# Inverse width DFT of a spectral convolution as four 64x64 TensorE tiles per product instead of one 128x128 product

## The reference

```python
xf = jnp.fft.rfft2(x, norm='forward')
top = jnp.einsum('bixy,ioxy->boxy', xf[:, :, :hm0, :hm1], w1)
bot = jnp.einsum('bixy,ioxy->boxy', xf[:, :, -hm0:, :hm1], w2)
out_fft = jnp.zeros((b, cout, h, w // 2 + 1), dtype=xf.dtype)
out_fft = out_fft.at[:, :, :hm0, :hm1].set(top)
out_fft = out_fft.at[:, :, -hm0:, :hm1].set(bot)
return jnp.fft.irfft2(out_fft, s=(h, w), norm='forward')
...
x = x + _L0_conv_ref(_ln_c(x), ...)
t = _to_tokens(x)
t = t + _L0_ffn_ref(_ln_t(t), ...)
```

## Time and profile before

| what | value |
|---|---|
| median of 3 runs (lowest, highest) | 591.72 us (589.74, 591.88) |
| the profiled execution, its own time | 587.68 us |
| its span in the trace | 585.9 us |
| mean granted TensorE clock | 0.962 |
| TensorE matmul busy | 528.1 us, 90% |
| VectorE busy | 344.6 us, 59% |
| ScalarE busy | 300.3 us, 51% |
| GpSimd busy | 114.7 us, 20% |

### The profile page before, as it was taken

How to read it: one execution, slowest core, us unless ns; L and a number is a source line. 1 busy time by engine, 2 the same in 40 slices (tenths; PEclk the granted TensorE clock), 3 DMA queues, 4 the chain that set the end, 5 groups by cost and what they waited for, 6 DMA issues and landing times.

```text
span 585.9 us, 25109 instructions
## 1 busy us (share of the span) xinstructions
PE 528.1 (90%) x11076; PEld 472.0 (81%) x11076; DVE 344.6 (59%) x815; ACT 300.3 (51%) x838; POOL 114.7 (20%) x240
## 2 busy tenths in 40 slices
PE   8978997999965999978999999979999999767997
PEld 8978987899964985767888999969998888656873
DVE  2758997734437936773545455435555455569726
ACT  4557997643377502454444444424445777667100
POOL 4000000000034000001333333553331033461000
PEclk9999998999998899998999999979999999978979
DMA  8940882070000000000000023430000244500007
GB/s 347 369 144 2 303 326 96 3 287 1 2 4 2 2 22 0 1 1 2 4 5 3 4 51 74 109 65 6 3 3 4 40 75 80 101 9 1 2 2 288
DMA packets 50260, 41.69 MB, mean 71 GB/s; under 512 B 44998, under 2 KB 45126, under 8 KB 48934
## 3 DMA queue, kind: packets, MB, share of 16 engines
q1 hardware_dynamic: 49304, 38.51, 20.5%
q0 software_dynamic: 704, 1.18, 0.9%
q10 hardware_dynamic: 144, 0.39, 0.2%
HBM read 27.49 MB, written 4.19 MB: 54 GB/s over the span
## 4 chain that ended last, share of the span: by engine, by line
PE 70%; DVE 16%; ACT 5%; POOL 4%; issue 3%; SPq 1%; DMA 0%; POOLq 0%; ACTq 0%; DVEq 0%
PE PS L755 38%; PE PS L724 5%; DVE RB L990 5%; PE PS L483 4%; PE PS L614 3%; PE PS L674 3%; PE PS L584 3%; PE PS L435 2%; PE PS L462 2%; PE PS L539 2%; POOL RE L393 2%; POOL RCD L396 2%; PE PS L492 2%; DVE sums L1032 1%; PE PS L684 1%
## 5 line engine op out<-in xcount | busy, mean ns | idle before, releaser
L755 PE MATMUL PS<-RE,conv_sb 128*64 128x64 f32 x6048 | 231.2, 230 | 4.3 <-DVE RE L1131 3.9
L755 PEld LDWEIGHTS PS<-RE,conv_sb 128*64 128x64 f32 x6048 | 209.1, 139 | 26.4 <-DVE RE L1131 4.6
L880 ACT COPY PS<-convb_sb 128x64 f32<-128x64 f32 x504 | 108.2, 215 | 112.8 <-DVE RE L1143 89.7
L1143 DVE SCALAR_TENSOR_TENSOR RE<-PS,RCD 128x64 f32<-128x64 f32 x252 | 56.7, 225 | 58.0 <-PE PS L755 50.4
L405 POOL COPY RCD<-RE 128x128 f32<-128x128 f32 x126 | 37.4, 297 | 154.3 <-DVE RE L1143 154.2
L1143 DVE SCALAR_TENSOR_TENSOR RE<-PS,RE 128x64 f32<-128x64 f32 x126 | 32.6, 259 | 28.3 <-PE PS L755 26.9
L1143 DVE SCALAR_TENSOR_TENSOR RE<-PS,RB 128x64 f32<-128x64 f32 x126 | 28.4, 225 | 28.1 <-PE PS L755 20.2
L818 ACT COPY RB<-PS 32x256 f32<-32x256 f32 x64 | 40.5, 633 | 7.5 <-PE PS L523 6.7
L990 DVE COPY RB<-PS 32x256 f32<-32x256 f32 x64 | 40.3, 630 | 5.7 <-PE PS L523 4.9
L539 PE MATMUL PS<-RE,RB 128*64 128x64 f32 x1024 | 33.3, 227 | 5.1 <-DVE RCD L999 2.5
L483 PE MATMUL PS<-warm 128*128 128x128 bf16 x468 | 34.3, 239 | 3.9 <-DVE warm L908 1.4
(11 more groups left out here) (116 smaller groups left out, 715.0 us busy)
## 6 DMA issues: line engine op xcount, KB each, us to landing
RE<-wspec SPq DMA_DIRECT2D x8, 2048.0 KB, 8.5
RA<-x_in SPq DMA_DIRECT2D x8, 512.0 KB, 7.4
RCD<-x_in SPq DMA_DIRECT2D x1, 4096.0 KB, 13.7
out<-RA SPq DMA_DIRECT2D x8, 512.0 KB, 2.9
RCD<-RB SPq DMA_DIRECT2D x58, 64.0 KB, 2.6
RE<-RCD SPq DMA_DIRECT2D x32, 80.0 KB, 2.6
conv_sb<-conv_w SPq DMA_DIRECT2D x1, 768.0 KB, 20.0
w_sb<-w SPq DMA_DIRECT2D x2, 264.0 KB
```

The lines of the kernel that those rows point to most:

```text
L755: m = pe.matmul(conv_bank(s, u, c)[o:o + OC], conv_sb[:, s, d, o:o + OC], prev, start=False, stop=(d == 2), skip_group_check=True)
L880: act.copy(banks_of, convb_sb[:, s:s + 1].unsqueeze(2).to_broadcast([P, c1 - c0, n])).then_inc(s_seed, 1)
L1143: dve.scalar_tensor_tensor(out=state[:, state_slot(s, u), b0:b1, 1:1 + HO], in0=conv_bank(s, u, c), scalar=0.0, in1=row_at(SRC[s], s, q, u ...
```

## The change

`dft_w_back` calls a new function `quad` in place of one 128x128 product. For each block it makes four products of 64x64: row half a of the block and of the table, column half o of the block. The zeros of the table are left out. Row half a now writes to bank a of the pair, so that the pair no longer holds whole blocks one after the other, but the first 64 pixels' columns of all eight blocks in one bank and the second in the other. The residual add reads the pair in that order and RC in the same order as before. Waits, signals and the order of the engines stay as they were.

```diff
+            def quad(bank, n, lhs, table):
+
+                for a in range(2):
+                    rows = slice(MO * a, MO * (a + 1))
+                    for o in range(2):
+                        cols = slice(MO * o, MO * (o + 1))
+                        m = pe.matmul(PS[cols, bank + a, MO * n:MO * (n + 1)], lhs[rows, cols], table[rows, rows],
+                                      start=True, stop=True)
+                return m
+
...
                 for n in range(8):
-                    m = pe.matmul(blk(dft_slot(g), n), blk(RB, 8 * g + n), inv_w, start=True, stop=True)
+                    m = quad(4 + 2 * (g % 2), n, blk(RB, 8 * g + n), inv_w)
                 m.then_inc(s_if1, 1)
...
             for g in range(8):
                 dve.wait_ge(s_if1, g + 1)
-                x1 = RC[:, 1024 * g:1024 * g + 1024]
-                dve.tensor_tensor(x1, dft_slot(g), x1, ALU.add).then_inc(s_res, 1)
+                x1 = RC[:, 1024 * g:1024 * g + 1024].rearrange("p (n a w) -> p n a w", a=2, w=W)
+                dve.tensor_tensor(x1, dft_slot(g).rearrange("p (a n w) -> p n a w", a=2, w=W), x1,
+                                  ALU.add).then_inc(s_res, 1)
```

## The result

The changed kernel takes 587.0 us (median of 20 runs, 583.37 to 589.39), the kernel before, timed beside it, 591.44 us (586.62 to 592.81). The medians lie 4.4 us apart. The ratio on record, which is not simply that of the medians, is 0.994 with an interval of 0.992 to 0.996: 3.5 us less, with 2.4 to 4.7 us in the interval, and that is what I go by. The forecast was 6.6 us.

A forecast was written before the change was run, and what follows sets the result against it. The prediction took TensorE to bound the stage; 5.2 us saved over groups 0 to 5 plus 1.45 us at the end made 6.6 us, so 591.7 - 6.6 = 585.1 us, range 581.0 to 589.0 us.

The forecast's parts named there:

- the floor per record: Rival in the group products: 0.0207 us is a floor of feeding records; 3.9 us saved, 587.8 us; chance 0.20, shared.
- What bounds the stage: First product to projection: TensorE bounds its 20.91 us, until ScalarE's drain (1.01 us per group) or VectorE's add (1.23) is next.
- 0.0146 us per record by the rule of columns: Group products: the larger column count, weights or moving, sets a round of four 64x64 tiles, 0.059 us.
- The gaps: Between products and turns in each group: 0.15 us after a turn stays; 0.20 us taken from products to a turn.
- No drain: Rival at switches between row and quarter tiles: gaps of 0.03 us, 1.7 us more saved, 583.4 us; chance 0.07.
- The add in runs of 64: VectorE's residual add, reading banks in runs of 64: nothing taken; at the strided add's cost, some 1.7 us.
- the end of the stage: Start of group 6 to the projection: 3.70 us instead of 5.15, 1.45 us saved, the add becoming the bound.
- TensorE must also be fed: Feeding 64 more records of each kind per group in the stage: nothing taken; one stop would eat 2.35 us.
- The clock: Rival in the stage: the granted clock falls to half, slower by 5.1 us, 596.8 us; chance 0.05.
- No overlap of the row halves: Rival in the group products: only column halves overlap, 0.029 us per record, gain gone, 592.1 us; chance 0.12, shared.
- a floor, or a single stop or fall of about 3 us: Joint case in the stage: floor of 0.0207 us per record, or one stop or clock fall; near 588 us, chance 0.20.

The follow-up runs named there:

- the mixed tiles: Changed kernel with groups 1, 3 and 5 as row tiles, 16 clock matmuls written as 4; stage 15.74 us, ratio 0.9938 to the kernel before.
- row tiles only: Changed kernel with two 64x128 row tiles per product in place of four 64x64 tiles; stage 18.84 us, ratio 0.9953 to the kernel before.
- the sweeps: Changed kernel plus ten sweeps of 64x64 tiles behind the last product, 64 or 96 moving columns, results unused; sweeps took some 18.5 us in both.
- group 4 or every second group put back: Changed kernel with group 4, or groups 0, 2, 4 and 6, back to 128x128 products; stage 15.91 or 17.59 us, ratio 0.9909 or 0.9953.
- 37 records fewer ahead: Changed kernel with 50 clock matmuls far ahead of the stage written as 13 longer ones; stage 16.79 us, ratio 0.9936 to the kernel before.

## Why the prediction was right, and where it was not

The forecast was faster, 585.1 us in a range of 581.0 to 589.0; the time is 587.0 us. That it lies in the range is in part luck: 3.5 us came of the 6.6 us of the sum, and the range reached up to 589.0 us for the floor per record, which did not come. By the steps of the prediction:

- **What bounds the stage**: right for the kernel before. Shortening the products shortened the stage, and neither drain nor add became the bound inside the loop.
- **0.0146 us per record by the rule of columns**: right. (1.16 - 0.218) / 63 = 0.0149 us, with a median record of 218 ns in the changed kernel. The floor of 0.0207 us does not exist for single records; that rival falls, though its 3.9 us is near the measured 3.5 us. Periods of 1.73 us rather than 2.1 us tell them apart. The row tiles confirm the rule a second time, with 128 columns of weights, to within 6%.
- **The gaps**: right. 1.09 us per group against 1.12 us forecast: 1.09 - 63 x 0.0149 = 0.15 us, less than my 0.20. No drain falls as a rival for this change: the turn still holds 0.64 us. The Trainium skill (TensorEngine Tiling (Array Packing), Key Properties) has TensorE drain at a change of tiling mode, and the trace agrees: 0.64 us for a turn between other forms, 0.50 us between row tiles.
- **The add in runs of 64**: right, 1.23 us as before, and so is the end of the stage where no stop disturbs it: from group 6 to the projection 158.58 - 154.90 = 3.68 us with the mixed tiles, 3.70 forecast. In the changed kernel it was 5.28 us, no better than the 5.15 us before: the stop in group 7 ate the whole 1.45 us.
- **TensorE must also be fed**: this is the term that failed. I took nothing and held one stop of 2.35 us for possible. It came to four stops, 4.3 us, which took about 4.1 of the 6.7 us that the stage would have gained. The error was in the reading. The stream of 128 records without a stop is 256 instructions, no longer than one block, and a group's wait followed behind it; it does not say whether the next block is there. The stop inside a group was there to be read, and I put it down to the busy DMA engines. In the stage here they were idle but for the instruction packets, and it stopped all the same. In the changed kernel the late stop is there again, after the same 114 records of a group, as it is with row tiles only and with the sweeps, whose streams differ from the one before by whole blocks of 128 records. In the kernel with quarter and row tiles, 108 records shorter than the changed one, it came after 93 records of a group, where the count gives 94:

```profile
512.44 0.55 PE L658 MATMUL PS<-proj,RA 64*64 64x96 f32 x14 [2.08 <-issue]
```

```profile
517.61 1.04 PE L675 MATMUL PS<-proj,RA 64*64 64x96 f32 x35 [1.34 <-issue]
```

So the late stop belongs to the same count. What the busy DMA engines add to it stays open: with group 4 or every second group put back, or 37 records fewer ahead, the count puts it after 34, 50 and 23 records of a group, and no stop is seen there. What would have told it: 160 instructions per 1.76 us are 256 in 2.8 us, while the projection's first 512 instructions, two streams with a wait for ScalarE between them, took 166.78 + 2.96 - 162.64 = 7.1 us before, 256 in 3.55 us; nothing there showed a quicker feed for more than one block. The second of the two streams:

```profile
166.78 2.96 PE L648 MATMUL PS<-proj,RCD 64*64 64x96 f32 x128 [1.27 <-ACT RA L851]
```

- **The clock**: it stayed at 1.00 through the stage (142.19 to 160.47 us); that rival did not come. Its row was read too simply: of the 106 records ahead of the fall about ten were clock matmuls of 128 columns, not tiny tiles.
- **No overlap of the row halves**: fell with the record time.

The chance for "a floor, or a single stop or fall of about 3 us" was the nearest to what came; the mechanism was feed, in several stops, with the forecast's record time under it.

What stays open: why a block takes 3.45 us at one time and 4.28 at another, and when the next is asked for. Not tested is whether the recording of the trace slows the feed: every time on record here comes with a span and a clock of its own, and none without. The Trainium skill (Runtime: NRT & Kernel Launch, Instruction fetch mechanics) describes blocks of 16 KiB, 256 instructions, of which the next is fetched while the current one is worked off, and calls the cost of a boundary mostly hidden. The trace agrees on the block and shows that it is not hidden here, where 256 instructions are worked off in less than 3.45 us block after block.

## What to carry to other kernels

A product split into smaller tiles is paid in instructions: before taking its time from columns, count the instructions per us that the stretch will ask of TensorE, over several hundred of them, against 256 per 3.45 to 4.28 us here. Where they are too many, split only part of the products, so that slow and quick groups alternate; five of eight groups in quarters and three in row tiles gave twice the saving in the stage (5.2 against 2.6 us), and seven of eight in quarters nearly as much (5.0 us). And an idle time put down to "issue" in the middle of a group is a finding; count the records from one such stop to the next.

## What was not expected of the hardware

- TensorE's instructions came in 16 KB packets, and in a stream of small products 256 of them took 3.45 to 4.28 us, with the DMA engines otherwise idle. Stops came every 126 to 128 records, whatever these computed.
- Where the stops fall depends on the length of the program ahead: 37 records fewer, some 90 us earlier, moved them by 36 or 37 records. The stage was 1.5 us shorter in that profile, of which the varying length of the stops may be a part.
- Row tiles of one form follow each other without a gap: a turn between row-tile products holds 0.50 instead of 0.64 us.
